# Scatter stage of a four-layer graph network: group totals in a PSUM bank of their own, in-group ranks made four groups ahead

## The chip, the cores and the metric

The kernel runs on one core of a Trainium2 chip. The metric is the device time of one execution in microseconds (us); lower is better. Engines are named as in the profile: PE (TensorE, matmuls; its weight loads are PEld), DVE (VectorE), ACT (ScalarE), POOL (GpSimd) and SP (SyncE). PSUM is the memory that matmuls write, here one tensor `acc` of eight banks of 512 fp32 columns.

## What is computed

Four message-passing layers on one graph of 3125 nodes and 53125 directed edges, all with 128 features. In the reference, cut to what matters here:

```python
edge_index = jnp.stack([src, dst])
h = jnp.maximum(_layernorm(x), 0.0)
x = x + _L0_gnn_ref(h, edge_index, edge_attr_128, ...)   # edge rows summed by src and by dst
x = x + _L1_gnn_ref(h, edge_index, edge_attr_128, ...)   # edge rows summed by dst
x = x + _L2_gnn_ref(h, edge_index, ...)                  # two graph convolutions
x = x + _L3_gnn_ref(h, edge_index, edge_attr_128, ...)   # a small network on every edge
```

`dst` is sorted and `src` is not. To sum the edge rows by `src`, the kernel first sorts them: each edge row of 128 fp32 goes to the table `rows_by_block` in DRAM, in the block of 128 nodes to which its source belongs. Its place in the block is the number of earlier edges with the same source block. This placing, and the counting of edges between nodes, are the scatter stage.

## The kernel before

The function `place_and_count` is the stage. 416 tiles of 128 edges each (one edge to a partition) are worked through in 104 groups of four tiles (`KC`), and each group in two pairs of two tiles (`PG` is 2). Nothing is scheduled by a planner: each engine has its own unrolled program, written by hand, and engines meet at semaphores (`ranked`, `based`, `pair_done` and so on). `x.wait_ge(s.h, s.at(n))` makes engine x wait until s has been raised n times, and every instruction behind it on that engine waits too.

For a group g:

- DVE, `which_block(g)` (L762 to L768): `block_hot`, for each of the four tiles a one-hot row over 26 blocks, in bf16. Two buffers, so the one of group g waits for `ranked.at(g)`, that is, for the ranks of group g-1.
- PE, `rank(g)` (L830 to L840): the ranks in PSUM at `R_AT`, bank 6. An fp32 matmul spreads `bases`, the running count of each block, over the four tiles and over a fifth piece of 26 columns; four bf16 matmuls (`shared`, L827) add each tile's counts to all later pieces; one with a triangular matrix (L840) adds the ranks inside a tile and raises `ranked`. The fifth piece ends as the total after the group.
- DVE, `own_rank(g)` (L770 to L773): multiplies the ranks by `block_hot` and raises `ranks_read`. `place(g)` and `place_whole(g)` reduce and cast them to four columns of `place_in_table`, and raise `placed`.
- ACT, `base_of_next(g)` (L729 to L731): copies the fifth piece to `bases` for the next group, and raises `based`. It waits for `ranks_read`, since DVE reads the same bank.
- POOL: four indirect DMAs (L707), one for each tile, that write the 128 rows of a tile to their places. They need `placed`, the key in the row (`staged`, by ACT's `key_in_row`) and the loaded row (`row_in`, by SP).

For a pair i: DVE makes `wide_hot` (`hots`, L759), ACT makes `low_hot` (`lows`, L724 and L727), PE multiplies them (L855) and the edge rows (L861), and DVE adds the result from PSUM to `between` and `by_dst` (`collect`, L791 and L793). Banks 0 to 5 hold three pairs, so PE is at most three pairs ahead of `collect`; `wide_hot` and `low_hot` have four buffers.

Each pair step of the three programs is short:

```python
for i in range(PAIRS):            # PE
    if c == 0 and g + 1 < GROUPS:
        rank(g + 1)
    ...                           # the pair's matmuls
for i in range(PAIRS + 2):        # DVE
    # place(g); hots(i); place_whole(g); which_block(g + 2); collect(i - 2); own_rank(g + 1)
```

The comment line stands for DVE's calls in their order; `place`, `place_whole` and `which_block` are made in the first pair of a group, `own_rank` in the second.

The stage after it sums the table block by block. Much later, in the last layer, POOL issues 416 further indirect DMAs, which gather rows (L1749).

## Time and profile before

| | |
|---|---|
| median of 3 runs | 2008.05 us (2004.0 to 2008.35) |
| profiled execution | 2016.29 us |
| its span, first to last instruction | 2014.3 us |
| scatter stage, first pair's matmul to POOL's last DMA | 24.0 to 708.6 us, 684.6 us |
| busy in the stage: PE, DVE, POOL, ACT | 500.8, 396.1, 400.4, 254.1 us |

The profile is one execution. Times in it are counted from the start of the span. An instruction's idle time stands in brackets behind it, with what ended it; "remote" means that the profile knows the semaphore's time but finds no instruction that ended near it, and "issue" that it finds no wait. The ends of matmuls in it are modelled. The TensorE clock is granted in full in the whole stage.

### The profile page before, as it was taken

How to read it: one execution, taken by the hardware profiler on the slowest of the kernel's cores; microseconds unless marked ns; L12 is line 12 of the kernel's file. 1: busy time of each engine (PE TensorE's matmuls, PEld its weight loads, DVE VectorE, ACT ScalarE, POOL GpSimd, SP SyncE). 2: the span in 40 equal slices, each digit the busy share in tenths (PEclk: the TensorE clock that was granted, in tenths of full speed). 3: DMA queues.
4: the chain of work that ended last, by engine and by line, in shares of the span. 5: the costliest groups of instructions: out<-in, count | busy, mean ns of one | idle time of the engine just before them, and what ended most of it. 6: DMA issues, size and time to landing. Idle time of an engine off the chain costs nothing. (4 is left out here: it accounts for less than half of the span.)

```text
span 2014.3 us, 29793 instructions
## 1 busy us (share of the span) xinstructions
PE 1418.1 (70%) x8157; PEld 1171.9 (58%) x8158; DVE 815.1 (40%) x2558; ACT 545.0 (27%) x1393; POOL 800.0 (40%) x844
## 2 busy tenths in 40 slices
PE   4777777777677678676769642666676767766789
PEld 3555555555555568653769431665666656665673
DVE  4566656556566556435331420222222222222230
ACT  5333333333333387011000120211121212121221
POOL 3566656555566500000000006454555555555500
PEclk9999999999999999978789665555555555555557
DMA  6222222222222167560000023333333333433401
GB/s 201 77 85 85 83 78 82 76 82 82 77 84 83 43 191 237 160 66 1 1 1 2 1 87 92 104 107 97 105 106 98 109 103 99 106 104 99 123 12 32
DMA packets 194193, 174.24 MB, mean 87 GB/s; under 512 B 45051, under 2 KB 166771, under 8 KB 193939
## 3 DMA queue, kind: packets, MB, share of 16 engines
q1 hardware_dynamic: 167444, 117.97, 21.1%
q0 software_dynamic: 26624, 54.79, 9.6%
q8 instruction: 55, 0.90, 0.2%
q14 instruction: 70, 0.57, 0.1%
HBM read 134.52 MB, written 38.15 MB: 86 GB/s over the span
## 5 line engine op out<-in xcount | busy, mean ns | idle before, releaser
L1749 POOL DMA_INDIRECT between<-p_table,src_g x416 | 394.0, 947 | 815.8 <-issue 628.7
L707 POOL DMA_INDIRECT rows_by_block<-h_t,mean_bc x312 | 300.2, 962 | 235.7 <-issue 109.4
L855 PE MATMUL acc<-n_nm 128*128 128x384 bf16 (+1 forms) x832 | 247.7, 453 | 183.8 <-DVE n_nm L759 90.2
L1831 PEld LDWEIGHTS acc<-between 128*128 128x128 f32 x832 | 217.6, 323 | 247.9 <-ACT between L1808 181.5
L1831 PE MATMUL acc<-between 128*128 128x24 f32 x832 | 210.9, 342 | 206.9 <-ACT between L1808 196.5
L1845 PE MATMUL acc<-w_msg,between 128*128 128x128 f32 x832 | 308.3, 474 | 0.0
L855 PEld LDWEIGHTS acc<-n_nm 128*128 128x128 bf16 x832 | 96.1, 134 | 264.3 <-issue 170.1
L1801 ACT ACTIVATE between<-acc 128x256 f32<-128x256 f32 x208 | 79.7, 383 | 609.7 <-remote 320.4
L1789 DVE TENSOR_TENSOR agg_sum<-agg_sum,acc 128x24 f32 x208 | 37.5, 180 | 510.4 <-remote 267.1
L1820 PE MATMUL acc<-ident,between 128*128 128x128 f32 x416 | 175.1, 422 | 62.8 <-issue 33.6
L1845 PEld LDWEIGHTS acc<-w_msg,between 128*128 128x128 f32 x832 | 215.1, 318 | 0.6
L791 DVE TENSOR_TENSOR between<-between,acc 128x600 f32 x208 | 161.8, 778 | 64.7 <-issue 55.2
L861 PEld LDWEIGHTS acc<-agg_sum,h_t 128*128 128x128 f32 x624 | 152.3, 334 | 4.5
L861 PE MATMUL acc<-agg_sum,h_t 128*128 128x24 f32 x624 | 143.6, 361 | 0.0
L759 DVE TENSOR_SCALAR n_nm<-iota_w,agg_sum 128x600 bf16<-128x600 f16 x416 | 143.4, 387 | 0.0
L724 ACT ACTIVATE away<-iota_b,agg_sum 128x128 bf16<-128x128 bf16 x416 | 140.8, 385 | 0.0
L1820 PEld LDWEIGHTS acc<-ident,between 128*128 128x128 f32 x416 | 95.0, 229 | 65.2 <-issue 34.9
L731 ACT ACTIVATE bases<-acc 1x26 f32<-1x26 f32 x104 | 18.9, 182 | 420.4 <-issue 234.6
L1062 PE MATMUL acc<-n_nm,h_t 128*128 128x128 f32 x882 | 111.4, 284 | 20.9 <-DVE n_nm L1028 20.3
L707 POOL DMA_INDIRECT rows_by_block<-agg_sum,mean_bc x104 | 100.2, 963 | 63.6 <-issue 42.2
L1466 PE MATMUL acc<-agg_sum,between 128*128 128x192 bf16 x1250 | 107.6, 251 | 22.4 <-DVE agg_sum L1450 22.4
L1062 PEld LDWEIGHTS acc<-n_nm,h_t 128*128 128x128 f32 x882 | 104.5, 196 | 27.8 <-DVE n_nm L1028 27.1
(182 smaller groups left out, 2056.1 us busy)
## 6 DMA issues: line engine op xcount, KB each, us to landing
h_t<-rows_by_block SPq DMA_DIRECT2D x73, 387.0 KB, 3.8
between<-in_edge_attr SPq DMA_DIRECT2D x207, 128.0 KB
h_t<-in_edge_attr SPq DMA_DIRECT2D x78, 256.0 KB
between<-in_dst SPq DMA_DIRECT2D x51, 288.0 KB
between<-p_table,src_g POOLq DMA_INDIRECT x416
agg_sum<-in_edge_attr SPq DMA_DIRECT2D x25, 256.0 KB
rows_by_block<-h_t,mean_bc POOLq DMA_INDIRECT x312
rows_by_block<-x_nm SPq DMA_DIRECT2D x1, 4644.0 KB, 16.0
```

Of the source, the lines that this page charges most:

```text
L707: pool.indirect_dma_start(rows_by_block, bass.IndirectOffsetOnAxis(ap=place_in_table[:, t:t + 1], axis=0), row_group(g)[:, j, :], None).th ...
L724: act.activation(away[:, h + j, :], iota_b[:, :], ACT.Abs, scale=-1.0, bias=lo_s[:, 2 * i + j:2 * i + j + 1])\
L759: ins = dve.tensor_scalar(wide_hot[:, i % HOTB * 2 + j, :], iota_w[:, :], key_w[:, t:t + 1], None, ALU.is_equal)
L791: dve.tensor_tensor(between[:, :, bass.ds(first, W)], between[:, :, bass.ds(first, W)], acc[:, o:o + NB * WS].rearrange("p (b w) -> p b w" ...
L855: pe.matmul(acc[:, to:to + (b1 - b0) * WS].rearrange("p (b w) -> p b w", w=WS)[:, :, 0:W], low_hot[:, h + j, :], wide_hot[:, h + j, b0 * W ...
L861: pe.matmul(acc[:, o2:o2 + W], row_group(g)[:, c + j, 0:D], win_hot[:, v + j, :], start=j == 0, stop=j == 1)
L1062: last = pe.matmul(acc[:, o:o + P], rows_in_block[:, q, j, 0:D], hot_in_block[:, q, j, :], start=is_first and j == 0, stop=is_last and j = ...
L1466: last = pe.matmul(acc[:, o:o + 3 * H2], counts[:, b, d * P:d * P + P], z_parts[:, b, :], start=b == 0, stop=b == NB - 1)
L1749: pool.indirect_dma_start(got[:, q, j * D:(j + 1) * D], None, p_table, bass.IndirectOffsetOnAxis(ap=src_g[:, n * G + j:n * G + j + 1], axi ...
L1820: last = pe.transpose(acc[:, o:o + P], rows[:, i, j, :], ident[:, :])
L1831: last = pe.matmul(acc[:, o:o + W], relued[:, i % MR, j, :], onehot[:, i * G + j, :], start=j == 0, stop=j == G - 1)
L1845: last = pe.matmul(acc[:, o:o + P], turned[:, i % MR, j * P:(j + 1) * P], w_msg[:, 2, :], start=False, stop=True)
```

## The change

The total after each group gets a bank of its own, `TOTAL_AT` (bank 7), and a chain of its own: `total(g)` on PE spreads the base over 26 columns with one fp32 matmul and adds the four tiles' counts with four bf16 matmuls of 26 columns, then raises a new semaphore, `totaled`; `base_of_next` waits for that in place of `ranks_read`. `bases` has four buffers. `rank(g)` loses the fifth piece and runs four groups ahead of the pairs, just ahead of a group's second pair; `total` runs five groups ahead, just ahead of the first. `block_hot` is made for four groups at once. Keys are put into the rows five groups ahead and places are made two groups ahead.

```diff
-AHEAD = 2
+KEYS_AHEAD = 5
+RANKS_AHEAD = 4
+HOTG = 4
...
-        bases = sb("bases", [1, 2, NK])
+        bases = sb("bases", [1, 4, NK])
...
-        block_hot = more_space.take([P, 2, KC, NK], BF16)
+        block_hot = more_space.take([P, 2, HOTG * KC, NK], BF16)
...
                     def base_of_next(g):
-                        act.wait_ge(ranks_read.h, ranks_read.at(g + 1))
-                        act.activation(bases[:, (g + 1) % 2, :], acc[0:1, R_AT + RANKS:R_AT + RANKS + NK], ACT.Copy).then_inc(based.h, 1)
-
-                    for g in range(AHEAD):
+                        act.wait_ge(totaled.h, totaled.at(g + 1))
+                        act.activation(bases[:, (g + 1) % 4, :], acc[0:1, TOTAL_AT:TOTAL_AT + NK], ACT.Copy).then_inc(based.h, 1)
+
+                    for g in range(RANKS_AHEAD + 1):
                         key_in_row(g)
-                    base_of_next(0)
+                        base_of_next(g)
                     for i in range(PAIRS):
                         lows(i)
                         g = i // PG
-                        if i % PG == 0 and g + AHEAD < GROUPS:
-                            key_in_row(g + AHEAD)
-                        if i % PG == 1 and g + 1 < GROUPS:
-                            base_of_next(g + 1)
+                        if i % PG == 0 and g + KEYS_AHEAD < GROUPS:
+                            key_in_row(g + KEYS_AHEAD)
+                        if i % PG == 1 and i >= 3 and g + RANKS_AHEAD < GROUPS:
+                            base_of_next(g + RANKS_AHEAD)
...
-                    def which_block(g):
-                        if g >= 2:
-
-                            dve.wait_ge(ranked.h, ranked.at(g))
...
+                    def which_blocks(m):
+                        if m >= 2:
+
+                            dve.wait_ge(ranked.h, ranked.at((m - 1) * HOTG))
...
-                    which_block(0)
-                    which_block(1)
-                    own_rank(0)
+                    which_blocks(0)
+                    which_blocks(1)
+                    for g in range(RANKS_AHEAD):
+                        hots(g)
+                        own_rank(g)
+                        place(g)
+                        place_whole(g)
                     for i in range(PAIRS + 2):
                         g = i // PG
-                        if i % PG == 0 and g < GROUPS:
-                            place(g)
-                        if i < PAIRS:
+                        if RANKS_AHEAD <= i < PAIRS:
                             hots(i)
-                        if i % PG == 0 and g < GROUPS:
-                            place_whole(g)
-                        if i % PG == 0 and g + AHEAD < GROUPS:
-                            which_block(g + AHEAD)
+                        if i >= 3 and i % PG == 0 and g + 2 < GROUPS:
+                            place(g + 2)
+                        if i % PG == 1 and g % HOTG == 1 and (g + 7) // HOTG < GROUPS // HOTG:
+                            which_blocks((g + 7) // HOTG)
                         if i >= 2:
                             collect(i - 2)
-                        if i % PG == 1 and g + 1 < GROUPS:
-                            own_rank(g + 1)
+                        if i >= 3 and i % PG == 0 and g + 2 < GROUPS:
+                            place_whole(g + 2)
+                        if i >= 3 and i % PG == 1 and g + 3 < GROUPS:
+                            own_rank(g + 3)
...
+                    def total(g):
+
+                        pe.wait_ge(blocks_hot.h, blocks_hot.at(g // HOTG + 1))
                         if g >= 1:
                             pe.wait_ge(based.h, based.at(g))
-                        h = g % 2
-                        pe.matmul(acc[:, R_AT:R_AT + RANKS + NK].rearrange("p (t k) -> p t k", k=NK), ones[0:1, 0:P],
-                                  bases[:, h:h + 1, :].broadcast_to([1, KC + 1, NK]), start=True, stop=False)
+                        pe.matmul(acc[:, TOTAL_AT:TOTAL_AT + NK], ones[0:1, 0:P], bases[:, g % 4, :], start=True, stop=False)
                         for j in range(KC):
-                            shared(h, j, j + 1, KC + 1)
...
+                            last = pe.matmul(acc[:, TOTAL_AT:TOTAL_AT + NK], ones_b[:, :], hot_of(g)[:, j, :], start=False, stop=j == KC - 1)
+                        last.then_inc(totaled.h, 1)
+
+                    def rank(g):
+
+                        if g >= 1:
+                            pe.wait_ge(based.h, based.at(g))
+                            pe.wait_ge(ranks_read.h, ranks_read.at(g))
...
-                        if c == 0 and g + 1 < GROUPS:
-                            rank(g + 1)
+                        if c == 0 and g + RANKS_AHEAD + 1 < GROUPS:
+                            total(g + RANKS_AHEAD + 1)
+                        if c > 0 and g + RANKS_AHEAD < GROUPS:
+                            rank(g + RANKS_AHEAD)
```

**PE, in the steady part.** Before, a group on PE reads as follows. L836 to L840 are the rank of the next group, L855 to L864 the pairs; `n_nm` holds the one-hots, `agg_sum` and `h_t` the block one-hots and the edge rows.

```order
L836 MATMUL acc<-bases,ones 128x130 [waits based_29,blocks_hot_32]
L827 MATMUL acc<-agg_sum,ones_b 128x104
L827 MATMUL acc<-agg_sum,ones_b 128x78
L827 MATMUL acc<-agg_sum,ones_b 128x52
L827 MATMUL acc<-agg_sum,ones_b 128x26
L840 MATMUL acc<-agg_sum,lower_b 128x104
L855 MATMUL acc<-n_nm 128x16x24 [waits taken_36,lows_made_31,hots_made_35]
```

The changed program has this at the same place, with the rank ahead of the second pair (L880 is now the pair's first matmul):

```order
L844 MATMUL acc<-bases,ones 128x26 [waits based_29,blocks_hot_32]
L846 MATMUL acc<-agg_sum,ones_b 128x26 x4
L880 MATMUL acc<-n_nm 128x16x24 [waits taken_37,lows_made_31,hots_made_33]
L880 MATMUL acc<-n_nm 128x16x24
L880 MATMUL acc<-n_nm 128x9x24 x2
L886 MATMUL acc<-agg_sum,h_t 128x24 [waits row_in4_12]
L886 MATMUL acc<-agg_sum,h_t 128x24
L889 MATMUL acc<-agg_sum,ones_b 128x24 x2
L854 MATMUL acc<-bases,ones 128x104 [waits ranks_read_35,based_29]
L857 MATMUL acc<-agg_sum,ones_b 128x78
L857 MATMUL acc<-agg_sum,ones_b 128x52
L857 MATMUL acc<-agg_sum,ones_b 128x26
```

One fp32 and four bf16 matmuls of 26 columns come in for one bf16 matmul, the rank moves behind the first pair, and it waits for `ranks_read`, which DVE raises.

**DVE, in the steady part.** Before, the first pair step of a group (L759 `hots`, L781 `place_whole`, L766 `which_block`, L785 to L793 `collect`):

```order
L759 TENSOR_SCALAR n_nm<-iota_w,agg_sum 128x600 [waits pair_done_16]
L759 TENSOR_SCALAR n_nm<-iota_w,agg_sum 128x600
L781 CAST mean_bc<-place_f 128x4 [waits place_made_34]
L766 TENSOR_TENSOR agg_sum<-iota,agg_sum 128x104 [waits ranked_33]
L785 TENSOR_LOAD win_i
L785 ISA x2
L791 REGISTER_ALU [waits taken_36,pair_done_16]
L791 TENSOR_TENSOR between<-between,acc 128x25x24
```

The same step in the changed program (L766 is now `hots`, L786 `place`, L794 to L802 `collect`, L790 `place_whole`):

```order
L766 TENSOR_SCALAR n_nm<-iota_w,agg_sum 128x600 [waits pair_done_16]
L766 TENSOR_SCALAR n_nm<-iota_w,agg_sum 128x600
L786 TENSOR_REDUCE place_f<-agg_sum 128x4 [waits ranks_read_35]
L794 TENSOR_LOAD win_i
L794 ISA x2
L800 REGISTER_ALU [waits taken_37,pair_done_16]
L800 TENSOR_TENSOR between<-between,acc 128x25x24
L802 ISA
L802 TENSOR_TENSOR by_dst<-by_dst,acc 128x2x24
L790 CAST mean_bc<-place_f 128x4 [waits place_made_36]
```

The wait for the newest rank is gone from the step; the cast that lets POOL start a group now stands behind a `collect`, which waits for `pair_done`.

## Rows read from the trace of the kernel before

**Rows 1.** The page, its first line.
```profile
span 2014.3 us, 29793 instructions
...
```

**Rows 2.** Scatter stage by engine: us, busy us (x instructions).
```profile
...
24.00:708.60 684.60, 500.75 (x2789) 387.88 (x2789) 396.13 (x1286) 254.13 (x825) 400.36 (x416) 1.00 0.27 81
...
```

**Rows 3.** Groups, scatter stage: busy us, mean ns, idle before, releasers.
```profile
...
L707 POOL DMA_INDIRECT rows_by_block<-h_t,mean_bc x312 | 300.2, 962 | 235.7 <-issue 109.4 <-ACT h_t L717 87.6 <-ACT agg_sum L717 33.7
...
L791 DVE TENSOR_TENSOR between<-between,acc 128x600 f32 x205 | 159.4, 778 | 61.5 <-issue 55.2 <-PE acc L864 6.2
...
L766 DVE TENSOR_TENSOR agg_sum<-iota,agg_sum 128x104 bf16<-128x104 f32 x102 | 27.3, 267 | 222.9 <-PE acc L840 117.2 <-remote 100.4 <-issue 5.2
...
```

**Rows 4.** Waits, scatter stage: us in total, times, longest us.
```profile
...
DVE agg_sum L766 <- PE acc L840: 117.2, 78, 2.5
...
DVE agg_sum L766 <- remote: 100.4, 21, 8.7
...
DVE between L791 <- PE acc L864: 6.2, 4, 3.9
...
```

**Rows 5.** Timeline, two groups: start us, us, instruction, idle before.
```profile
...
399.81 0.80 PE L836 MATMUL acc<-bases,ones 1*128 1x130 f32 x2
...
401.07 0.27 DVE L766 TENSOR_TENSOR agg_sum<-iota,agg_sum 128x104 bf16<-128x104 f32 x1 [1.26 <-PE acc L840]
...
405.27 0.80 PE L836 MATMUL acc<-bases,ones 1*128 1x130 f32 x2
...
406.00 0.40 PE L827 MATMUL acc<-agg_sum,ones_b 128*128 128x104 bf16 x4
...
406.24 0.25 PE L840 MATMUL acc<-agg_sum,lower_b 128*128 128x104 bf16 x1
...
406.28 1.20 PE L855 MATMUL acc<-n_nm 128*128 128x384 bf16 x4
...
407.16 0.27 DVE L766 TENSOR_TENSOR agg_sum<-iota,agg_sum 128x104 bf16<-128x104 f32 x1 [1.54 <-PE acc L840]
407.27 0.92 PE L861 MATMUL acc<-agg_sum,h_t 128*128 128x24 f32 x4
...
408.02 0.22 PE L864 MATMUL acc<-agg_sum,ones_b 128*128 128x24 bf16 x2
...
408.77 0.66 DVE L759 TENSOR_SCALAR n_nm<-iota_w,agg_sum 128x600 bf16<-128x600 f16 x2
...
409.49 1.18 PE L855 MATMUL acc<-n_nm 128*128 128x384 bf16 x4 [1.24 <-DVE n_nm L759]
...
411.36 0.80 PE L836 MATMUL acc<-bases,ones 1*128 1x130 f32 x2
...
```

**Rows 6.** Timeline of the next group, same columns.
```profile
...
412.33 0.25 PE L840 MATMUL acc<-agg_sum,lower_b 128*128 128x104 bf16 x1
...
416.70 0.27 DVE L766 TENSOR_TENSOR agg_sum<-iota,agg_sum 128x104 bf16<-128x104 f32 x1 [5.28 <-remote]
...
```

**Rows 7.** Timeline of another group, same columns.
```profile
...
362.94 0.25 PE L840 MATMUL acc<-agg_sum,lower_b 128*128 128x104 bf16 x1
...
367.52 0.96 POOL L707 DMA_INDIRECT rows_by_block<-h_t,mean_bc  x1 [0.30 <-issue]
370.75 0.27 DVE L766 TENSOR_TENSOR agg_sum<-iota,agg_sum 128x104 bf16<-128x104 f32 x1 [8.40 <-remote]
...
375.76 0.96 POOL L707 DMA_INDIRECT rows_by_block<-h_t,mean_bc  x1 [7.28 <-ACT agg_sum L717]
...
```

**Rows 8.** Timeline of the later gather stage, same columns.
```profile
...
1253.56 0.94 POOL L1749 DMA_INDIRECT between<-p_table,src_g  x1 [0.30 <-issue]
1255.81 0.38 ACT L1801 ACTIVATE between<-acc 128x256 f32<-128x256 f32 x1 [22.00 <-remote]
...
```

**Rows 9.** Timeline of the scatter stage's start, same columns.
```profile
...
20.96 0.79 PE L836 MATMUL acc<-bases,ones 1*128 1x130 f32 x2 [10.79 <-DVE agg_sum L766]
...
23.96 1.16 PE L855 MATMUL acc<-n_nm 128*128 128x384 bf16 x4
...
```

More of the change, by code:

```diff
@@ L579, in build @@
         blocks_hot = signal("blocks_hot")
+        totaled = signal("totaled")
         ranked = signal("ranked")
@@ L668, in at_bank, with hot_of @@
                 return i % PRING * 2 * BANK
-            R_AT = PRING * 2 * BANK
+            R_AT, TOTAL_AT = PRING * 2 * BANK, (PRING * 2 + 1) * BANK
             RANKS = KC * NK
+            def hot_of(g):
+                c = g % HOTG * KC
+                return block_hot[:, g // HOTG % 2, c:c + KC, :]
             def row_group(g):
@@ L824, in _ @@
                 @on(block.tensor)
                 def _(pe):
-                    def shared(h, j, t0, t1):
-                        return pe.matmul(acc[:, R_AT + t0 * NK:R_AT + t1 * NK].rearrange("p (t k) -> p t k", k=NK), ones_b[:, :],
-                                         block_hot[:, h, j:j + 1, :].broadcast_to([P, t1 - t0, NK]), start=False, stop=False)
-                    def rank(g):
-                        pe.wait_ge(blocks_hot.h, blocks_hot.at(g + 1))
+                    def total(g):
+                        pe.wait_ge(blocks_hot.h, blocks_hot.at(g // HOTG + 1))
@@ L840, in rank @@
-                        pe.matmul(acc[:, R_AT:R_AT + RANKS], lower_b[:, :], block_hot[:, h, :, :].rearrange("p t k -> p (t k)"), start=False, stop=True)                          .then_inc(ranked.h, 1)
-                    rank(0)
+                            last = pe.matmul(acc[:, TOTAL_AT:TOTAL_AT + NK], ones_b[:, :], hot_of(g)[:, j, :], start=False, stop=j == KC - 1)
[4 more added lines that the diff above has]
+                            pe.wait_ge(ranks_read.h, ranks_read.at(g))
+                        pe.matmul(acc[:, R_AT:R_AT + RANKS].rearrange("p (t k) -> p t k", k=NK), ones[0:1, 0:P],
+                                  bases[:, g % 4:g % 4 + 1, :].broadcast_to([1, KC, NK]), start=True, stop=False)
+                        for j in range(KC - 1):
+                            pe.matmul(acc[:, R_AT + (j + 1) * NK:R_AT + RANKS].rearrange("p (t k) -> p t k", k=NK), ones_b[:, :],
+                                      hot_of(g)[:, j:j + 1, :].broadcast_to([P, KC - 1 - j, NK]), start=False, stop=False)
+                        pe.matmul(acc[:, R_AT:R_AT + RANKS], lower_b[:, :], hot_of(g).rearrange("p t k -> p (t k)"), start=False, stop=True)\
+                          .then_inc(ranked.h, 1)
@@ L843, in _ @@
+                    for g in range(RANKS_AHEAD):
+                        total(g)
+                        rank(g)
+                    total(RANKS_AHEAD)
                     for i in range(PAIRS):
                         g, q, c = i // PG, i // PG % ROWG, i % PG * 2
-                        if c == 0 and g + 1 < GROUPS:
-                            rank(g + 1)
+                        if c == 0 and g + RANKS_AHEAD + 1 < GROUPS:
+                            total(g + RANKS_AHEAD + 1)
+                        if c > 0 and g + RANKS_AHEAD < GROUPS:
+                            rank(g + RANKS_AHEAD)
@@ L872, in place_and_count @@
                 s.passed(PAIRS)
-            for s in (staged, ranked, based, blocks_hot, ranks_read, place_made, placed):
+            for s in (staged, totaled, ranked, based, ranks_read, place_made, placed):
                 s.passed(GROUPS)
+            blocks_hot.passed(GROUPS // HOTG)
             away_made.passed(EC)
```

12 lines of the change are left out of this document (7 added, 5 removed).

## The prediction

> **What bounds the kernel now.** I first read the page: one execution spans 2014.3 us [rows 1], reported as 2016.29 us, 8.2 us above the median of the runs, 2008.05 us. I make the sums against the profiled execution and move the difference to the median. A change within 0.2% (4 us) is about what a measurement of this kernel can't tell from none.
>
> The busy times of the scatter stage come next. It lasts 684.6 us, 6.58 us for each of 104 groups. POOL is busy 400.4 us, DVE 396.1 us [rows 2], so neither fills it; a busy PE says little. POOL's DMA takes 0.96 us and the next follows 0.30 us later [rows 3, 7], so four cost 5.04 us a group, 524 us in all: a floor at 77% of the stage.
>
> Then the groups and the waits: DVE stands idle ahead of `which_block` (L766) for 222.9 us [rows 3]. 78 of those waits end with the rank matmul L840, 117.2 us; 21 are "remote", 100.4 us. Ahead of `collect` DVE hardly waits for a pair (6.2 us) [rows 4]. So the rank signal paces the loop.
>
> The timeline shows the loop. A clean group takes 5.46 us, from L836 at 399.81 to L836 at 405.27, and in it DVE waits 1.26 us. The loop is: the rank is done, DVE makes `block_hot`, collects, makes the next one-hots (408.77), and only then does PE start the second pair (409.49), having stood 1.25 us since 408.24, the end of the first [rows 5]. In other groups the rank's record ends at 412.58 (412.33 + 0.25) but DVE is let go only at 416.70 [rows 6], or it ends at 363.19 (362.94 + 0.25) and DVE goes on at 370.75, 2.3 us after POOL's last DMA of a run ended (367.52 + 0.96 = 368.48) [rows 7]. The same is seen in the gather stage: ACT waits 22.00 us for PE while POOL issues DMAs back to back, and is released at 1255.81, 1.3 us after the last one ended (1253.56 + 0.94) [rows 8]. So PE's signals reach the others late while POOL issues without a pause. I read this as a hold on the signal, since PE's records go on.
>
> How much is lateness: 102 waits at the clean 1.26 us are 128.5 us; the other 94.4 us are lateness. The 21 remote waits average 4.78 us, 3.52 us late each, 73.9 us together; the rest are late by 0.24 us on average. The stage is then 104 x 5.46 = 568 us, 94 us lateness, and 23 us of start, end and waits elsewhere.
>
> **The change part by part.**
>
> *DVE no longer waits for the newest rank.* `which_blocks` waits for a rank four groups old. Its 416 columns cost between one and four times 0.267 us [rows 3] in place of four such; DVE has 2.8 us a group to spare, so this counts as nothing. The 1.26 us wait goes, and PE's 1.25 us with it.
>
> *PE does more.* Its own work in a group now: rank 405.27 to 406.28, 1.01 us; first pair to 408.24, 1.96 us; second pair 409.49 to 411.36, 1.87 us [rows 5]; 4.84 us. `total` adds an fp32 matmul of 26 columns. No row has it with one row of weights: its cost lies between half of the four-record L861 (0.92 / 2 = 0.46 us, 24 columns) and L836 with 130 columns (405.27 to 406.00, 0.73 us); I take the low end, since 26 columns are nearest to 24. Four bf16 matmuls of 26 columns cost between 0.22 us (two of L864) and 0.40 us (four of L827, wider) [rows 5]; I take 0.30. One of L827 goes, 0.10 us. Net 0.66 us, bounds 0.48 and 1.05. PE needs 5.5 us a group (5.3 to 5.9). So the clean group gains nothing: 5.5 against 5.46, 104 x 0.04 = 4 us lost. All gain must come from lateness that no longer stops anyone.
>
> The Trainium skill (TensorE: Matmul & The Clock Gate, section Back-to-back issue gap) puts any matmul of 1 to 64 columns at one floor of about 25 ns; four would cost 0.10 us, and the stage's sum would be 21 us lower, but the rows of L827 and L864 are dearer, and I stay with them.
>
> *New waits.* PE's `rank` waits for `ranks_read`, which `own_rank` raises behind the collect of the second pair of the group before. Behind it on PE are the second pair and all later ones. After that earlier pair PE still has a `total` and a first pair, 0.66 + 1.96 = 2.6 us; DVE needs a collect (0.78 us) [rows 3], the short `by_dst` add, `own_rank` (a pass of the rank's size, 0.27 us) and the wakes, about 1.3 us. So a signal may be 1.3 us late at no cost. `total` waits for ACT's copy of the total before, which has nearly a group's time; the copy stands behind ACT's `lows`. ACT's `key_in_row` now waits for a scatter three groups back, not six, which POOL has issued long before unless it falls behind by two groups. The places are two groups ahead, so POOL no longer stands right behind DVE's cast; SP's loads keep their waits.
>
> *What remains of the lateness.* With 1.3 us of cover the 78 small ones vanish, and the 21 cost 3.52 - 1.3 = 2.2 us each, 47 us.
>
> *Start.* The first pair begins 3.0 us after the first rank matmul [rows 9]. Now four ranks (each about 1.01 + 0.3 for DVE + 0.66 for the total, 2.0 us) and up to 1 us for the wider one-hot stand ahead: 10 us, 7 more.
>
> Sum: 104 x 5.5 = 572, plus 47, plus the 23 of elsewhere, plus 7 = 649 us, against 684.6: 36 us less. 2016.3 - 36 = 1980 us profiled, 1972 us as a median. With PE at 5.3 and 5.9 us and cover between 0.8 and 2 us this case runs from 1940 to 2010.
>
> **The rivals.**
>
> *The hold takes its place (slower).* The signals are late because POOL runs without a pause, and the change lets POOL start a group earlier. The old critical signal, the rank, came just as POOL began a group (POOL's pause before); the new critical ones, the two pairs, come in the midst of its four DMAs. If they are let through about once a group, PE has stopped at `total` until ACT has done its `lows` and copy, about 1.4 us behind the release, and then needs its 5.5 us: 6.9 us a group, 104 x 6.9 + 30 = 748 us, 63 more, 2071 us. If one group in three still passes cleanly: 6.43 us, 699 us, 2022 us. I take 2045 as its middle. It decides from (684.6 - 30) / 104 = 6.29 us a group. For it: the 8.4 us wait came when POOL ran two groups without a pause [rows 7], and the gather stage, with deep buffers, shows the longest hold [rows 8]. Against it: DVE now waits for an older signal than before, so a single hold stops less.
>
> *All lateness is covered.* 572 + 30 = 602 us, 83 less: 1925 us. It needs holds that don't grow with POOL's load. The Trainium skill (SBUF — State Buffer, section Who interferes with whom) says that PE and ACT never wait on anyone; by that rule the lateness would not be POOL's doing, and this case would be likelier. The rows speak against it: both long waits end only behind the last DMA of a POOL run [rows 7, 8].
>
> *PE is dearer.* At the upper bound, 5.9 us: 614 + 47 + 30 = 691 us, 2014 us, which is no change or just slower.
>
> **How the numbers follow.** First case 0.42, hold 0.38, PE dearer 0.12, all covered 0.08. The likeliest is 1972. Leaving out the fully covered case and the dear end of the hold, the range is 1930 to 2065, and the first case's own is 1940 to 2010. Faster: 0.42 + 0.08 less a little that the first case gives to no change, 0.48; same, from its upper part and the dear PE, 0.10; slower, the hold and the rest of the dear PE, 0.42.
>
> **What would show it.** The wait ahead of the block one-hots gone; fp32 matmuls of the total near 0.46 us for a pair of records; PE 5.5 us a group with its idle time ended by `ranks_read` or by the one-hots in some twenty groups only; POOL's pauses below 0.5 us. Wrong would be: DVE waiting for pair signals ("remote") at `collect` for over 150 us, PE idle at its first matmul of `total`, or POOL runs of eight and more DMAs with DVE let go only behind them.

## The result, and the profile after

The changed kernel takes 2013.58 us (median of 12 runs, 1995.41 to 2021.92), the kernel before 2003.39 us (12 runs): a ratio of 1.0055, 95% interval 1.0029 to 1.008. It is a little slower, where 1972 us and a gain were forecast. One of the five runs of `before_plain_b` below took 2267.69 us and is left out of its ratio. Its profiled execution took 2013.21 us; its page begins with:

```profile
span 2011.4 us, 30858 instructions
...
```

That of before took 2016.29 us, 12.9 us above the median of its kernel, so the two traces show how the work runs, but not in which stage the typical run loses its 10 us. In them the scatters run from 24.8 to 702.3 us (before: 24.7 to 708.6), DVE's last collect ends at 712.4 us (before 713.6), and POOL's gathers take 709.3 us (before 711.2).

The groups of the scatter stage after, to be held against [rows 3] (us busy, mean ns, idle before and what ended it):

```profile
...
L714 POOL DMA_INDIRECT rows_by_block<-h_t,mean_bc x312 | 305.8, 980 | 221.8 <-issue 92.1 <-ACT h_t L724 85.8 <-ACT agg_sum L724 22.5
...
L800 DVE TENSOR_TENSOR between<-between,acc 128x600 f32 x208 | 162.3, 780 | 314.9 <-remote 185.6 <-PE acc L889 119.0 <-issue 9.2
...
L854 PE MATMUL acc<-bases,ones 1*128 1x104 f32 x208 | 76.7, 469 | 111.4 <-DVE agg_sum L781 59.4 <-ACT bases L738 30.7 <-issue 21.3
...
L844 PE MATMUL acc<-bases,ones 1*128 1x26 f32 x208 | 64.5, 396 | 18.6 <-DVE agg_sum L774 11.1 <-ACT bases L738 6.4 <-issue 0.9
...
```

The 222.9 us ahead of the block one-hots are gone. In their place DVE stands 314.9 us ahead of `collect` (L800; L791 before: 61.5 us), and PE 111.4 us ahead of the rank (L854), behind whose wait for `ranks_read` the pairs stand. The waits of the stage:

```profile
...
DVE between L800 <- remote: 185.6, 40, 10.8
...
DVE between L800 <- PE acc L889: 119.0, 71, 5.2
...
PE acc L854 <- DVE agg_sum L781: 59.4, 30, 3.3
...
```

40 remote waits are there now where 21 were [rows 4], the longest 10.8 us (8.7 before). The timeline shows a clean group and a held one:

```profile
...
404.23 0.62 PE L844 MATMUL acc<-bases,ones 1*128 1x26 f32 x2
...
409.54 0.62 PE L844 MATMUL acc<-bases,ones 1*128 1x26 f32 x2
...
412.50 1.07 POOL L714 DMA_INDIRECT rows_by_block<-h_t,mean_bc  x1 [1.84 <-ACT agg_sum L724]
...
416.46 0.22 PE L889 MATMUL acc<-agg_sum,ones_b 128*128 128x24 bf16 x2
...
416.88 0.78 DVE L800 TENSOR_TENSOR between<-between,acc 128x600 f32 x1 [0.66 <-PE acc L889]
...
419.00 0.22 PE L889 MATMUL acc<-agg_sum,ones_b 128*128 128x24 bf16 x2
...
421.47 0.96 POOL L714 DMA_INDIRECT rows_by_block<-h_t,mean_bc  x1 [0.30 <-issue]
...
421.77 0.22 PE L889 MATMUL acc<-agg_sum,ones_b 128*128 128x24 bf16 x2
...
424.05 0.78 DVE L800 TENSOR_TENSOR between<-between,acc 128x600 f32 x1 [5.36 <-remote]
...
```

A clean group takes 5.31 us (404.23 to 409.54). From 412.50 POOL issues eight DMAs, until 422.43. The pair that ends at 416.68 is still collected at 416.88; the next, which ends at 419.22, only at 424.05, 1.6 us behind the end of the run, and meanwhile PE has run on to the last pair that its banks allow. The 40 remote waits average 4.64 us, the 21 of before 4.78: there are twice as many, not longer ones. Counted over the scatters, with a pause where the next DMA starts over 0.55 us behind the last: before, 99 runs, 89 of them of four DMAs, with pauses of 1.91 us on average; after, 54 runs, 39 of them of eight, with pauses of 3.01 us. Seven steps of 1.28 us, the eighth DMA's 0.98 and a pause are 12.95 us for two groups, 6.5 us a group; over all scatters it is 6.52 us, where it was 6.58.

### The profile page after: what moved, and what is told of

It reads as the page before. It is cut to its first block and busy times, and to the rows that moved or that the text cites. A ratio compares the mean times of both kernels' runs of the same rounds, so it can differ in the third digit from the quotient of the medians.

```text
span 2011.4 us, 30858 instructions
## 1 busy us (share of the span) xinstructions
PE 1471.6 (73%) x8677; PEld 1225.0 (61%) x8678; DVE 790.1 (39%) x2480; ACT 554.5 (28%) x1393; POOL 807.9 (40%) x844
## 5 line engine op out<-in xcount | busy, mean ns | idle before, releaser
L714 POOL DMA_INDIRECT rows_by_block<-h_t,mean_bc x312 | 305.8, 980 | 221.8 <-issue 92.1
L800 DVE TENSOR_TENSOR between<-between,acc 128x600 f32 x208 | 162.3, 780 | 314.9 <-remote 185.6
L880 PE MATMUL acc<-n_nm 128*128 128x384 bf16 (+1 forms) x832 | 247.2, 450 | 8.2 <-DVE n_nm L766 6.1
L854 PE MATMUL acc<-bases,ones 1*128 1x104 f32 x208 | 76.7, 469 | 111.4 <-DVE agg_sum L781 59.4
L880 PEld LDWEIGHTS acc<-n_nm 128*128 128x128 bf16 x832 | 95.5, 132 | 80.0 <-issue 73.5
L766 DVE TENSOR_SCALAR n_nm<-iota_w,agg_sum 128x600 bf16<-128x600 f16 x416 | 140.8, 382 | 0.0
L854 PEld LDWEIGHTS acc<-bases,ones 1*128 1x128 f32 x208 | 51.7, 307 | 117.2 <-ACT bases L738 58.3
```

The source lines that it names most:

```text
L714: pool.indirect_dma_start(rows_by_block, bass.IndirectOffsetOnAxis(ap=place_in_table[:, t:t + 1], axis=0), row_group(g)[:, j, :], None).th ...
L766: ins = dve.tensor_scalar(wide_hot[:, i % HOTB * 2 + j, :], iota_w[:, :], key_w[:, t:t + 1], None, ALU.is_equal)
L800: dve.tensor_tensor(between[:, :, bass.ds(first, W)], between[:, :, bass.ds(first, W)], acc[:, o:o + NB * WS].rearrange("p (b w) -> p b w" ...
L854: pe.matmul(acc[:, R_AT:R_AT + RANKS].rearrange("p (t k) -> p t k", k=NK), ones[0:1, 0:P], bases[:, g % 4:g % 4 + 1, :].broadcast_to([1, K ...
L880: pe.matmul(acc[:, to:to + (b1 - b0) * WS].rearrange("p (b w) -> p b w", w=WS)[:, :, 0:W], low_hot[:, h + j, :], wide_hot[:, h + j, b0 * W ...
```

## The experiments

The chips turned out to have two conditions, and one and the same chip showed both at different times. In one, "held" below, the kernel before takes 2003 to 2024 us (medians): so it was in the comparison above, and in three of the nine sets of runs that follow. In the other, "free", it takes 1682 to 1686 us. The granted clock is the same by stage: 1.00 in the scatter stage and 0.50 in the gather stage, in the held and in the free trace of the kernel before. Each experiment is compared with runs of the kernel before made next to it. Where no ratio stands, the kernel's time is a single execution.

How late a signal is, is counted below from the end of the last matmul of its kind that had ended when the semaphore event came; PE may have gone on meanwhile, so this is the least that the signal can be late. Held traces lack some of the events.

| kernel | condition | us | before beside it | ratio (95%) |
|---|---|---|---|---|
| before_plain | free | 1675.9 | 1683.7 | 0.9956 (0.994 to 0.9972) |
| after_plain | free | 1662.9 | 1683.7 | 0.9873 (0.9858 to 0.9888) |
| after_castfirst | free | 1662.8 | 1683.7 | 0.9869 (0.9853 to 0.9884) |
| before_hot4 | free | 1645.6 | 1683.7 | 0.9773 (0.9759 to 0.9786) |
| before_again | free | 1684.5 | 1685.1 | |
| after_again | free | 1663.3 | 1685.1 | 0.987 (0.9854 to 0.9887) |
| hot4_plus_total | free | 1675.8 | 1683.0 | 0.9956 (0.9942 to 0.9971) |
| before_hot4_b | free | 1644.3 | 1683.0 | 0.9772 (0.9752 to 0.9791) |
| after_plain_b | free | 1663.3 | 1683.0 | 0.9882 (0.9859 to 0.9906) |
| before_plain_b | free | 1677.1 | 1684.0 | 0.9956 (0.9938 to 0.9973) |
| before_rank_late | held | 2073.5 | 2024.4 | 1.0243 (1.0226 to 1.0261) |
| after_all_late | held | 2039.9 | 2024.4 | 1.0091 (1.0072 to 1.0109) |
| hot4_quarters | free | 1847.4 | 1686.0 | |
| after_quarters | free | 1836.3 | 1686.0 | |
| hot4_quarters_b | held | 2113.6 | 2013.1 | |
| hot4_gap_quarters | free | 1748.7 | 1682.3 | |
| hot4_gap | free | 1746.0 | 1682.3 | 1.0381 (1.0364 to 1.0399) |
| hot4_gap_quarters_b | held | 1961.6 | 2012.2 | |

**Both kernels as they are.**

> The kernel before, unchanged, for its trace. On the chip of the first four runs it took 1683.7 us, 320 us less than in the comparison of the prediction, and their traces hold no remote waits. Hold theory: wherever it takes about 1684 us its PE signals come 0.01 us behind the matmuls and POOL still issues in runs of four; wherever it takes about 2003 us they come up to 8 us late, as shown. Rival (the chip is faster in everything, clock or DMA): the signals are equally late in proportion, and single instructions are shorter.

> The changed kernel, unchanged. Hold theory: where before takes about 1684 us, nothing is held, each group is bound by PE at 5.3 us in place of a loop of 5.46 us, and it ends 20 us (1.2%) sooner; where before takes about 2003 us, it is 0.5% slower as measured. Rival (PE's added work and the wait for the ranks read cancel the gain everywhere): within 5 us of before on any chip.

Free, the change gains 1.3%. In the kernel before DVE now waits ahead of L766 only for the rank's own time: 101 waits, none remote,

```profile
...
DVE agg_sum L766 <- PE acc L840: 108.5, 101, 2.7
...
```

and a rank that ends at 303.18 lets DVE go at 303.22 (timeline):

```profile
...
302.93 0.25 PE L840 MATMUL acc<-agg_sum,lower_b 128*128 128x104 bf16 x1
...
303.22 0.27 DVE L766 TENSOR_TENSOR agg_sum<-iota,agg_sum 128x104 bf16<-128x104 f32 x1 [1.15 <-PE acc L840]
...
```

So single instructions last as long as in the held traces (the rank's last matmul 0.25 us, a scatter 0.96 us), and only the signals differ: over the trace's semaphore events, none of the 208 of the pairs comes over 0.02 us behind a matmul's end, while of the 161 that the held trace has, 96 come over 0.3 us behind, up to 6.2 us. The scatters end at 593.2 in place of 708.6 us, and the gathers take 520.7 in place of 711.2 us. A group goes at 5.45 us, the prediction's clean one (5.46). That POOL would still issue in runs of four was wrong: 36 of its 53 runs are of eight, with no signal late. The changed kernel has no remote wait,

```profile
...
DVE between L800 <- PE acc L889: 166.9, 202, 3.5
...
```

and PE in it never stands: every group takes 5.31 us.

```profile
...
301.05 0.62 PE L844 MATMUL acc<-bases,ones 1*128 1x26 f32 x2
...
306.36 0.62 PE L844 MATMUL acc<-bases,ones 1*128 1x26 f32 x2
...
```

**Plain DMAs in place of the scatters.**

```diff
-                            pool.indirect_dma_start(rows_by_block, bass.IndirectOffsetOnAxis(...), row_group(g)[:, j, :], None)...
+                            pool.dma_start(rows_by_block[slot * P:(slot + 1) * P, :], row_group(g)[:, j, :])...
```

> The kernel before, with POOL's 416 indirect scatters replaced by plain DMAs of the same rows to fixed places (so the order inside a block is not the reference's, the bytes are). Hold theory (PE's signals reach the other engines late because POOL issues indirect DMAs without a pause): waits marked remote vanish, every group is clean at 5.46 us, the stage takes 104 x 5.46 + 23 = 590 us, 95 us less, about 1910 us in all. Rival (the loop of rank, DVE and PE sets 6.58 us whatever POOL does): under 20 us less.

> The changed kernel with the same replacement. Hold theory: signals on time, the stage is bound by PE at the 5.31 us that its clean group shows (404.23 to 409.54): 104 x 5.31 + 30 = 582 us, a little under the same edit of the kernel before, 1900 us in all. Rival (PE's added work or its wait for the ranks read is what ate the gain): it stays at 6.4 us a group and above 1980 us, and is slower than the same edit of the kernel before by more than 20 us.

> The changed kernel with plain DMAs in place of the scatters, again. Where before takes about 1684 us: 1663 us again. Where before takes about 2003 us, hold theory: signals of the scatter stage on time and the stage at 5.3 us a group, so about 115 us less than the changed kernel, with the gather stage unchanged. Rival: something else than POOL's DMAs makes that chip's signals late, and they stay late in this stage.

> The kernel before with plain DMAs in place of the scatters, on a further chip. Where before takes about 1684 us: 1676 us again. Where before takes about 2003 us, hold theory: about 110 us less than before, with the signals of the scatter stage on time and those of the gather stage still late. Rival (that chip's PE signals are late whatever POOL does): within 30 us of before.

All four were free, so they tell only that the scatters cost little there: 7 to 8 us in the kernel before, nothing in the changed one (1663.3 us as it is), which is bound by PE.

**The cast ahead of collect.**

```diff
+                        if i >= 3 and i % PG == 0 and g + 2 < GROUPS:
+                            place_whole(g + 2)
                         if i >= 2:
                             collect(i - 2)
-                        if i >= 3 and i % PG == 0 and g + 2 < GROUPS:
-                            place_whole(g + 2)
```

> The changed kernel with place_whole ahead of collect in DVE's pair step. Hold theory: POOL's run ends because the cast stands behind a collect that waits for a held signal; with the cast ahead, POOL's 54 pauses of 3.0 us lose the collect (0.98 us) or there are fewer of them: 30 to 55 us less than the changed kernel. Rival (a longer POOL run only holds the signals longer, so the pauses grow as they get fewer): within 10 us of the changed kernel. Rival (PE is the bound): no change.

Free, it is the changed kernel (0.9869 against 0.987), as PE is the bound there. Held, it wasn't tried.

**More buffers alone.** `block_hot` of the kernel before gets four buffers, which are read as `g % 4`, and nothing else changes:

```diff
-        block_hot = more_space.take([P, 2, KC, NK], BF16)
+        block_hot = more_space.take([P, 4, KC, NK], BF16)
...
-                        if g >= 2:
-                            dve.wait_ge(ranked.h, ranked.at(g))
+                        if g >= 4:
+                            dve.wait_ge(ranked.h, ranked.at(g - 2))
```

> The kernel before with four buffers of block_hot, so that which_block waits for a rank two groups older; nothing is added on PE. Hold theory: the wait ahead of which_block vanishes (222.9 us), and comes back ahead of own_rank and collect; 0 to 25 us less than before. Rival (the added matmuls and the longer start of the changed kernel cancel a real gain): 36 us less or more, since here the gain comes without them.

> The kernel before with four buffers of block_hot, again, as the neighbour of the run above. Where before takes about 1684 us: 1645 us again, POOL in one run of 416 DMAs, 5.10 us a group. Where before takes about 2003 us, hold theory: 0 to 25 us less than before, the waits moved to own_rank and collect; or slower, if POOL's longer runs hold the pairs' signals as in the changed kernel.

Free, this small part of the change gains 2.3%, against 1.3% for the whole. POOL issues all 416 scatters, each 0.3 us behind the last (the waits of the stage):

```profile
...
POOL rows_by_block L707 <- issue: 121.8, 400, 0.3
...
```

5.10 us a group is POOL's floor, and PE needs less, 4.67 us (timeline, two places):

```profile
...
69.64 0.80 PE L836 MATMUL acc<-bases,ones 1*128 1x130 f32 x2
...
74.31 0.80 PE L836 MATMUL acc<-bases,ones 1*128 1x130 f32 x2
...
```

```profile
...
345.88 0.80 PE L836 MATMUL acc<-bases,ones 1*128 1x130 f32 x2
...
350.55 0.80 PE L836 MATMUL acc<-bases,ones 1*128 1x130 f32 x2
...
```

**The total's price.** Into that kernel come the five matmuls of `total`, ahead of a group's second pair:

```diff
+                        if c > 0 and g + 1 < GROUPS:
+                            pe.matmul(acc[:, spare:spare + NK], ones[0:1, 0:P], bases[:, (g + 1) % 2, :], start=True, stop=False)
+                            for j in range(KC):
+                                pe.matmul(acc[:, spare:spare + NK], ones_b[:, :], block_hot[:, (g + 1) % 4, j, :], ...)
```

> The kernel before with four buffers of block_hot, and on PE, ahead of a group's second pair, the five matmuls of the changed kernel's total once more into a free bank, read by nobody. If the changed kernel stays behind the four-buffer kernel (1662.8 to 1645.6 us on one chip) because its total makes PE the bound, this one comes to PE's 5.3 us a group and 1655 to 1668 us. Rival (its order or its longer start is what costs, PE's added work is hidden): within 4 us of the four-buffer kernel. Where the kernel before takes about 2003 us the added work changes little beside the held signals.

```profile
...
430.90 0.80 PE L836 MATMUL acc<-bases,ones 1*128 1x130 f32 x2
...
433.81 0.62 PE L849 MATMUL acc<-bases,ones 1*128 1x26 f32 x2
...
434.36 0.28 PE L851 MATMUL acc<-agg_sum,ones_b 128*128 128x26 bf16 x4
...
434.49 1.16 PE L860 MATMUL acc<-n_nm 128*128 128x384 bf16 x4
...
436.34 0.80 PE L836 MATMUL acc<-bases,ones 1*128 1x130 f32 x2
...
```

A group takes 5.44 us (430.90 to 436.34), 0.77 us more than 4.67 us: 0.55 for the fp32 matmul (433.81 to 434.36), 0.13 for the four bf16 ones, and 0.09 for the step from the pair before. The kernel loses 31 us: PE is the bound. That is more than the forecast allowed, since the old rank with its fifth piece is still there too.

**Signals made late by hand.** The rank's signal is raised by the last row matmul of the pair behind it. In the changed kernel total and rank are treated so, and each pair's signal is raised by the last matmul of the next pair (the last two lines).

```diff
-                            rank(g + 1)
+                            rank(g + 1, False)      # its last matmul raises nothing
...
                             last = pe.matmul(acc[:, o2:o2 + W], row_group(g)[:, c + j, 0:D], ...)
+                        if c == 0 and g + 1 < GROUPS:
+                            last.then_inc(ranked.h, 1)
...
-                        last.then_inc(pair_done.h, 1)
+                        if i > 0:
+                            last.then_inc(pair_done.h, 1 if i < PAIRS - 1 else 2)
```

> The kernel before, with the rank's signal raised not by the rank's last matmul but by the last row matmul of the pair behind it, 1.9 us later (406.28 to 408.19 in rows 5). The wait ahead of which_block stands in the loop, so each group gets 1.9 us longer: 104 x 1.9 = 198 us, about 1880 us where the kernel before takes 1684. Rival (the wait has slack that the profile doesn't show): under 50 us.

> The changed kernel with every PE signal of the steady part late: total and rank are raised by the last row matmul of the pair behind them (1.9 us later), each pair by the last matmul of the next pair (2.5 to 3.0 us later). If the changed kernel has the slack that the prediction gave it, and more (a pair and a rank or total, 2.5 us), it stays within 10 us of 1663 us where nothing else is late; what cost it its gain on the first chip is then lateness beyond a pair. Rival (any lateness of the pairs' signals stops it, since collect and the rank's wait stand behind them): 1 to 2 us a group, 100 to 200 us more.

These runs were held. The kernel before loses 49 us, not 198: the late signal takes the place of lateness that was there. Its trace has 68 events of the rank in the stage, none over 0.2 us behind the matmul that now raises them, and a group takes 7.17 us (median distance of L836's starts), 1.72 more than the free 5.45. So here the 1.9 us put in by hand cost nearly their full length, as the loop of the prediction has it.

The changed kernel was forecast to stay within 10 us of its free time where nothing else is late. Its scatter stage doesn't: the last scatter ends at 726.0 us, free at 570.7. In that stage hardly anything but the lateness put in by hand is left (22 of the 139 pair events in the trace are over 0.3 us behind the matmul that raises them, and POOL is back at 94 runs of four, with pauses of 1.99 us), and 86 of the 97 groups between 40 and 700 us take the same 6.69 us, 1.38 more than 5.31:

```profile
...
400.73 0.69 ACT L731 ACTIVATE away<-iota_b,agg_sum 128x128 bf16<-128x128 bf16 x2 [1.20 <-PE acc L895]
...
401.87 0.16 ACT L738 ACTIVATE bases<-acc 1x26 f32<-1x26 f32 x1
...
402.03 0.72 PE L855 MATMUL acc<-bases,ones 1*128 1x104 f32 x2 [1.34 <-ACT bases L738]
...
404.77 0.62 PE L844 MATMUL acc<-bases,ones 1*128 1x26 f32 x2
...
411.46 0.62 PE L844 MATMUL acc<-bases,ones 1*128 1x26 f32 x2
...
```

ACT's `lows` waits for the late pair, its copy of the base stands behind `lows`, and PE's rank (L855) waits for the copy. The waits of the stage:

```profile
...
DVE between L800 <- PE acc L895: 163.0, 128, 3.4
...
PE acc L855 <- ACT bases L738: 120.8, 89, 2.1
...
DVE between L800 <- remote: 22.0, 2, 18.0
```

In the groups around these lines a pair ends at 404.84 us and its signal is raised at 407.38, 2.54 us later; PE waits 1.34 us of that. So on this path about 1.2 us of lateness are covered (an estimate from these times), and a lateness of about one pair does cost the changed kernel time, as the rival of the expectation has it (1 to 2 us a group): 104 x 1.38 = 144 us over its free pace. In the whole time little of it shows: the ratio to the kernel before is 1.0091, and that of the unaltered changed kernel, in another set of runs, 1.0055, with overlapping intervals. Here too the lateness put in takes the place of what was there.

In both traces the signals of the stage come mostly on time behind the matmuls that raise them, although the runs were held and POOL issues in runs of four (96 of 106 and 94 of 104). In the kernel before it does so too (89 of 99), and there 96 of 161 were late. So the length of POOL's runs alone doesn't decide it.

**Four conditions in one trace.** To compare within one execution, POOL's work differs between four quarters of 26 groups. The diff is that of the four-buffer kernel; in the changed kernel (`after_quarters`) the third quarter has the cast ahead of `collect` in place of a pause. The rows that the second quarter didn't place are written by 104 scatters behind the last group, so the whole times are longer and aren't compared.

```diff
+                            if g // 26 in [1]:
+                                pool.dma_start(rows_by_block[NB * CAP + t * P:NB * CAP + (t + 1) * P, :], row_group(g)[:, j, :])...
+                                continue
                             pool.indirect_dma_start(...)
+                            if g // 26 in [3]:
+                                rest(1)      # a memset of 256 columns, and a wait for it
+                        if g // 26 in [2]:
+                            rest(4)
```

> The four-buffer kernel with POOL's work unlike in four quarters of 26 groups: scatters as they are; plain DMAs to a spare region; scatters with a pause of about 1.4 us after each four; scatters with a pause of about 0.35 us after each one. The rows of the second quarter's places are filled with other rows behind the last group (104 scatters, some 130 us more). Where before takes about 1684 us: 5.1, 4.9, 6.5 and 6.5 us a group, every PE signal 0.01 us behind its matmul. Where before takes over 2000 us, hold theory: the first quarter 6 to 6.6 us a group with late signals, the second 4.9 us with none late (that is the test), the third with fewer late than the first, the fourth with signals still late if only a pause of over 1 us lets them pass, on time if any pause does. Rival (that chip's PE signals are late whatever POOL does): the second quarter late as the others.

> The changed kernel in quarters of 26 groups: scatters as they are; plain DMAs; scatters with DVE's place_whole ahead of collect; scatters with a pause of about 0.35 us after each one (second quarter's places filled behind the last group as above). Where before takes about 1684 us: 5.3, 5.3, 5.3 and 6.5 us a group. Where before takes over 2000 us, hold theory: first quarter 6.6 us, second 5.3 with no late signal, third 6.1 to 6.6 (a collect less in each of POOL's pauses, if the runs don't grow), fourth as it was or better. Rival as above.

> The quarters of the four-buffer kernel on another chip. Where before takes about 1684 us: 4.5, 4.4, 5.5 and 6.9 us a group between the pairs' ends, as in the run before. Where before takes over 2000 us, hold theory: first quarter 6 to 6.6 us with late signals, second 4.4 with none late, third with fewer late, fourth late unless any pause lets them pass. Rival: the second quarter is late as the others.

The first two were free. PE's groups took 5.31, 5.31, 5.31 and 5.37 us in the changed kernel; POOL, in the four-buffer kernel, issued a group in 5.12 us, in 7.11 us with the pause after each four, in 6.91 us with one after each DMA, and PE went 4.67 us a group until POOL's slower quarters held it. The third was held. The waits of its first quarter, scatters as they are:

```profile
...
DVE agg_sum L797 <- remote: 34.3, 9, 4.7
...
DVE between L816 <- remote: 20.4, 9, 10.5
DVE between L816 <- PE acc L889: 17.3, 5, 5.7
...
```

and of its second, plain DMAs:

```profile
...
DVE between L816 <- PE acc L889: 8.6, 27, 0.5
...
DVE agg_sum L797 <- PE acc L865: 2.8, 15, 0.5
...
```

| quarter, held | pair signals in the trace | over 0.3 us late | latest | POOL, us a group |
|---|---|---|---|---|
| scatters as they are | 45 | 29 | 5.9 us | 6.57 |
| plain DMAs | 52 | 0 | 0.01 us | |
| pause of 1.5 us after each four | 39 | 14 | 1.6 us | 7.13 |
| pause of 0.33 us after each | 37 | 2 | 0.3 us | 6.93 |

In the same execution, the signals are late beside scatters and on time beside plain DMAs of as many rows, and late again in the quarter behind. So in the held condition the scatters cause the lateness; which of their properties does (how POOL makes them, or where they write) isn't separated. The four-buffer kernel's first quarter takes 6.57 us a group, the kernel before 6.54 there: held, more buffers alone gain nothing.

**How small a pause does.** All scatters stay. The quarters have a memset of one column, and a wait for it, after each DMA; after every second; 256 columns after every second; and after every fourth. `hot4_gap` is the first throughout.

```diff
+                            pool.memset(pause[:, 0:cols], 0.0).then_inc(paused.h, 1)
+                            pool.wait_ge(paused.h, paused.at(rests[0]))
```

> The four-buffer kernel, all scatters as they are, with POOL's pause unlike in four quarters of 26 groups: a memset of one column and a wait for it (about 0.1 us) after each DMA; the same after every second; 0.35 us after every second; 0.35 us after every fourth. Where before takes about 1684 us: 5.3, 5.2, 5.7 and 5.5 us a group for POOL, all signals on time. Where before takes over 2000 us, hold theory: the fourth and the second quarter stay near 6.5 us, since whole runs of DMAs still hold the signals; the third comes to 5.8 to 6.2; the first shows whether 0.1 us between DMAs already lets a signal pass (then 5.4 us). Rival (a signal needs a pause of over 1 us): all at 6.5 or more.

> The four-buffer kernel with the one-column pause after each DMA throughout. Where before takes about 1684 us: 530 us of POOL get 416 x 0.1 = 40 us longer, 1685 us, no gain over before. Where before takes over 2000 us: if so short a pause lets a signal pass, 5.4 us a group and about 120 us less than before; if not, within 20 us of before or slower.

> The same quarters on another draw. Where before takes about 1684 us: POOL at 6.1, 5.9, 6.3 and 6.0 us a group as in the run before. Where before takes over 2000 us: no quarter under 6 us, and the question is whether signals are late at all in the first (0.1 us after each DMA), second and fourth.

`hot4_gap` takes 1746.0 us free, where 1685 was forecast: the pause costs more than its memset. Behind it the next scatter starts after 0.28 us, where 0.30 stood before, but at a group's first one after 0.83 us (timeline of `hot4_gap`):

```profile
...
302.60 0.11 POOL L715 MEMSET pause<- 128x1 f32 x1
...
302.99 0.96 POOL L710 DMA_INDIRECT rows_by_block<-h_t,mean_bc  x1 [0.28 <-POOL pause L715]
...
303.95 0.11 POOL L715 MEMSET pause<- 128x1 f32 x1
...
304.89 1.08 POOL L710 DMA_INDIRECT rows_by_block<-agg_sum,mean_bc  x1 [0.83 <-POOL pause L715]
...
```

So POOL takes 6.06, 5.94, 6.31 and 5.97 us a group, free, and 6.09, 5.92, 6.34 and 5.97 us held. Signals still come late, 25 of 41, 27 of 43, 13 of 42 and 4 of 27 of the pairs, but by 3.7 us at most, and POOL's pace no longer depends on them: 50.6 us less than the kernel before (2.5%, one execution of each). Free, the same pauses cost 66 us, 3.9%. No version beats both kernels in both conditions: four buffers alone do when free and are level with before, by one quarter, when held; with pauses they win only when held.

## Why the prediction failed

*What bounds the kernel.* Right, and now shown: where signals are on time the kernel before goes at 5.45 us a group (5.46 was read), and the rest of its 6.58 is lateness that POOL's scatters cause in the held condition. That it isn't the program's alone, but a condition that comes and goes, the profile of one execution couldn't tell.

*DVE's wait and PE's work.* The wait for the rank is gone. The total costs 0.77 us where 0.46 + 0.30 = 0.76 was taken, but only because two errors cancel: the fp32 matmul takes 0.55, the four bf16 ones 0.13. PE's other work, 4.67 us, is 0.17 less than the 4.84 read off [rows 5], so a group takes 5.31 us and not 5.5. The low bound of 5.3 rests on a slip: the prediction's own low terms, 0.46 + 0.22 - 0.10, are 0.58 and not 0.48, which gives 5.42, above what was measured. The rule of the Trainium skill (TensorE: Matmul & The Clock Gate, section Back-to-back issue gap), by which four small matmuls cost 0.10 us, was set aside for two dearer rows; the trace's 0.13 is nearer to it. The bf16 matmuls of those rows overlap what is behind them, and their durations can't be taken for their cost; the distance of starts can.

*Start.* 7 us more were forecast; the first pair starts at 31.3 in place of 23.96 us.

*The step that failed* is "What remains of the lateness. With 1.3 us of cover the 78 small ones vanish, and the 21 cost 3.52 - 1.3 = 2.2 us each, 47 us". The cover is of about that size (1.2 us, estimated from `after_all_late`), though the path that first uses it up there runs over ACT's copy of the base, which the prediction counted as having nearly a group's time. What was wrong is the number of holds, which was taken over from the old program. DVE now has 40 remote waits at `collect`, 185.6 us, where 21 ahead of the block one-hots made 100.4, and they stand in front of the read of the ranks and of POOL's cast, for which PE's rank and POOL wait. From its first matmul of a pair to the last (680.1 us) PE stands 130 us: 111.4 at the rank, 6.5 at the total, 8.2 at the pairs' first matmuls and 4.5 at others; of the 111.4, 59.4 us end with DVE's read of the ranks and 30.7 with ACT's copy. 104 x 5.31 + 130 = 682 us is the stage from its first pair to its last collect (31.3 to 712.4, 681 us). Forecast were 47 us and the 23 of elsewhere, 60 us less; the 104 x (5.5 - 5.31) = 20 us that PE gave back don't make up for it. POOL's runs went from four DMAs to eight along with it. Whether they are why the holds became more isn't shown: free, the kernel before issues in eights with no signal late, and in `before_rank_late`, held, signals are on time beside runs of four.

*The rivals.* "The hold takes its place", with 0.38, is what came, by the mechanism it names: DVE lets go at `collect` behind runs of eight, remote waits of 185.6 us, over the 150 that were given as its mark. Its price, 2045 us, was too high: it stands for 6.43 to 6.9 us a group and 30 us more for start and end, and the stage took 678 us (24.0 to 702.3), 6.5 us a group with both in it. "PE is dearer" gives 2014 us, the measured median, by chance: PE needs 5.31 us a group and not 5.9. "All lateness is covered" has 602 us for the stage; free, the changed kernel's scatters take 546 us (24.8 to 570.7), for another reason: there is no lateness. The Trainium skill (SBUF — State Buffer, section Who interferes with whom) has it, of the ports of SBUF, that PE and ACT never wait on anyone. The traces don't speak against it, since PE's matmuls last as long held as free (L880's mean is 0.450 and 0.451 us); but it doesn't reach to PE's signals, and the prediction leaned on it for those. In the quarters they come up to 5.9 us late beside scatters, and 0.01 us beside plain DMAs.

*Left open:* what puts a chip into the held condition; why a signal is held beside scatters there; why there were more holds in the changed kernel; whether the earlier cast helps when held; and in which stage the typical held run of the changed kernel loses its 10 us, since the profiled run of before was an unusually slow one.

## What to carry to other kernels

Where an engine's waits are late beside another engine's work, don't carry their number over to the changed program: with one wait taken away they came back at the next semaphore, 40 where there were 21. To learn how much lateness a program covers, make its signals late by hand and read the distance of groups in the trace, not the whole time, in which it can replace lateness that was there. When one trace can hold several versions of a loop in turn, one execution compares them under the same condition, which separate runs can't promise. And try the smallest part of a change by itself: two more buffers gave 2.3% free, where buffers, a second total and a longer lead gave 1.3%.

## What the runs showed of the hardware

The same program took 1684 or 2003 to 2024 us with the same granted clock in each stage (1.00 in the scatters', 0.50 in the gathers'; the means, 0.78 and 0.76, differ because the gather stage lasts longer when held) and the same durations of single instructions; PE's signals came within 0.02 us or many us late (pairs up to 6.5 us, ranks up to 13.3 us in the changed kernel's stage), only in the stages with indirect DMAs (outside them the held trace of the kernel before has 231 events of PE's signals, none over 0.02 us late), and the kernels' order of merit changed with it.

PE's group took 4.67 us at a granted clock of 1.00 (2.4 GHz) and at 0.50 (1.2 GHz), as the two timelines of `before_hot4` above and this view of its stretches show (us, busy us by engine, then the granted clock):

```profile
...
60.00:100.00 40.00, 40.00 (x247) 31.63 (x246) 33.67 (x109) 20.89 (x69) 30.35 (x32) 1.00 0.34 98
345.00:362.00 17.00, 16.18 (x96) 12.79 (x95) 13.03 (x43) 7.51 (x25) 13.04 (x14) 0.50 0.37 105
...
```

These small matmuls, with their weight loads, thus took as long at either level. Why the clock fell there, from about 100 us on, stays open: PE was busy all of the 40 us before, but so it was in `after_again` (545.3 of 546 us), at 1.00 throughout.
